# Gate scores taken from the output product, in an attention and expert kernel on one Trainium2 core

## What is computed

```python
x = x + xattn(layernorm(x), ctx, w_q, w_k, w_v, w_o, b_o)     # 16 heads of 64
y = layernorm(x)                                              # 64*128 tokens of 256
raw = softmax(y @ gate)                                       # 8 experts
g = the two largest of raw, divided by their sum
x = x + sum over those two experts e of g[e] * (relu(y @ W1[e] + b1[e]) @ W2[e] + b2[e])
```

## Time and profile before

| | |
|---|---|
| median of three runs | 1673.28 us (1673.21 to 1675.51) |
| profiled execution | 1680.6 us, span 1678.8 us, mean granted clock 0.995 |
| PE busy | 1638.5 us (98%) |
| DVE, ACT, POOL busy | 1249.7, 1219.1, 801.8 us (74%, 73%, 48%) |
| DMA | mean 85 GB/s |

### The profile page before, as it was taken

One profiled execution on the slowest core, in us unless ns is written; L12 is line 12 of the kernel. 1 busy time (PEld: TensorE's weight loads), 2 busy tenths in 40 slices (PEclk: granted clock), 3 DMA queues, 4 the chain that ended last, 5 costly groups with the idle time before them and its releaser, 6 DMA issues.

```text
span 1678.8 us, 45315 instructions
## 1 busy us (share of the span) xinstructions
PE 1638.5 (98%) x13932; PEld 1547.4 (92%) x13933; DVE 1249.7 (74%) x3302; ACT 1219.1 (73%) x3547; POOL 801.8 (48%) x888
## 2 busy tenths in 40 slices
PE   6999999999999999999999999999899999999997
PEld 6899999999999999999999999998899999999997
DVE  6777777777777777777777777776778777777775
ACT  6777777777777777777777777777666677777774
POOL 3334444444444444444444444444436555555555
PEclk9999999999999999999999999999999999999999
DMA  7121111122111111221111112211489655555554
GB/s 237 47 64 63 57 57 57 57 79 76 65 63 57 57 57 57 87 72 62 63 57 57 57 57 88 72 63 48 133 270 278 131 84 86 89 86 88 84 87 60
DMA packets 105755, 142.96 MB, mean 85 GB/s; under 512 B 12464, under 2 KB 88368, under 8 KB 105584
## 3 DMA queue, kind: packets, MB, share of 16 engines
q1 hardware_dynamic: 60672, 86.91, 15.8%
q0 software_dynamic: 26816, 37.32, 12.4%
q10 hardware_dynamic: 18224, 18.19, 3.9%
HBM read 75.00 MB, written 67.38 MB: 85 GB/s over the span
## 4 chain that ended last, share of the span: by engine, by line
issue 46%; POOL 20%; PE 12%; DVE 8%; DMA 6%; DVEq 3%; ACT 2%; POOLq 2%; ACTq 0%; SPq 0%
POOL lists L600 7%; PE bank_a L1284 6%; DMA out<-stage_room,number 5%; POOL prob L607 5%; DVE hid L1200 3%; POOL rstd L586 2%; DVE stage_room L1217 2%; POOL stage_room L633 2%; POOL stage_room L629 2%; PE bank_s L1284 2%; PE bank_t L1291 1%; PE bank_v L1317 1%; POOL out L669 1%; DVEq L1212 1%; POOLq L663 1%
## 5 line engine op out<-in xcount | busy, mean ns | idle before, releaser
L607 POOL TENSOR_TENSOR prob<-prob,inv 128x512 f32<-128x512 f32 x256 | 268.9, 1051 | 630.8 <-DVE inv L896 617.4
L713 ACT ACTIVATE prob<-bank_s,low 128x128 f32<-128x128 f32 x1024 | 363.1, 367 | 170.6 <-DVE low L891 129.0
L891 DVE TENSOR_REDUCE low<-bank_s 128x4 f32<-128x512 f32 x256 | 176.5, 690 | 253.3 <-PE bank_s L1284 253.1
L669 POOL DMA_INDIRECT out<-stage_room,number x142 | 232.0, 1634 | 53.5 <-issue 52.6
L713 ACT ACTIVATION_READ_ACCUMULATOR prob<-bank_s,low 128x1 f32 x1024 | 208.4, 204 | 0.0
L1291 PE MATMUL bank_t<-ident,prob 128*128 128x128 f32 x1024 | 164.5, 283 | 12.1 <-POOL prob L607 11.0
L919 DVE TENSOR_TENSOR kt_l<-bank_a,kt_h 64x512 fp32r<-64x512 f32 x256 | 173.2, 677 | 1.7
L822 ACT ACTIVATE hidt_h<-hid 128x512 fp32r<-128x512 f32 x142 | 89.8, 632 | 109.8 <-DVE hid L1200 105.2
L1284 PE MATMUL bank_s<-kt_l,qt_h 128*128 128x256 f32 x512 | 166.2, 325 | 0.0
L751 ACT ACTIVATE ot_h<-bank_v 128x512 fp32r<-128x512 f32 x128 | 76.5, 598 | 114.6 <-PE bank_v L1317 112.7
L706 ACT ACTIVATE probt<-bank_t 128x512 f32<-128x512 f32 x256 | 152.9, 597 | 8.3 <-PE bank_t L1291 7.0
(11 more groups left out here) (210 smaller groups left out, 5313.3 us busy)
## 6 DMA issues: line engine op xcount, KB each, us to landing
stage_room<-lists ACTq DMA_DIRECT2D x67, 265.0 KB
halves<-stage_room SPq DMA_DIRECT2D x32, 512.0 KB, 3.7
homes<-halves SPq DMA_DIRECT2D x8, 2048.0 KB, 10.1
xin<-in_x SPq DMA_DIRECT2D x32, 256.0 KB
stage_room<-in_x SPq DMA_DIRECT2D x32, 256.0 KB, 3.1
stage_room<-in_w SPq DMA_DIRECT2D x32, 256.0 KB, 3.8
out<-stage_room SPq DMA_DIRECT2D x32, 256.0 KB, 2.2
cin<-in_ctx SPq DMA_DIRECT2D x32, 128.0 KB
```

Of the source, the lines that this page charges most:

```text
L607: pool.tensor_tensor(prob[:, n % 4, :, :], prob[:, n % 4, :, :], wide(inv[:, n % 4, :], P), ALU.mult).then_inc(s_norm.sem, 1)
L669: pool.indirect_dma_start(out, bass.IndirectOffsetOnAxis(ap=number[:, u, b:b + 1], axis=0), ysum[:, u, b, :], None, compute_op=ALU.add).th ...
L713: e = act.activation(prob[:, n % 4, h, :], bank_s[n % 2][:, h * P:(h + 1) * P], ACT.Exp, bias=low[:, n % 4, h:h + 1], scale=-1.0, accum_ou ...
L891: dve.tensor_reduce(low[:, n % 4, :], bank_s[n % 2][:, :].rearrange("p (h k) -> p h k", h=4), AX.X, ALU.min).then_inc(s_low.sem, 1)
```

## The change

The gate scores of a pair are linear in the sums, up to the two numbers of the layer norm. The gate is first centred (`gate_c`, its column mean subtracted), so that the mean of a row drops out, and the scores become rstd times (x1 · gate_c). x1 is the output product plus the tokens plus the bias, so the kernel computes w_o · gate_c once (`wo_gate`, made in pass 0 in the place of `o1`, from a transposed w_o that a new 1 MB DMA brings) and hangs it to w_o as eight more columns: `o0` and `o1` have 264 moving columns for 256. The part of the tokens comes from eight small float32r products in the new `f0`, at the end of slot 7: stationary the 128x128 parts of `xt`, moving 16 columns of the gate's high and low parts. DVE rescales it (`x_gate`), POOL adds the bias's part.

```diff
 A_SLOTS:
-        [("q10", CUR), ("k10", CUR), ("l0", EARLIER)],
+        [("q10", CUR), ("k10", CUR)],
         [("o0", PREV)],
         [("k11", CUR), ("q11", CUR)],
-        [("f0", EARLIER), ("o1", PREV)],
-        [("v10", CUR), ("v11", CUR), ("t0", NEXT), ("t1", NEXT)],
+        [("o1", FROM0), ("t0", NEXT)],
+        [("v10", CUR), ("v11", CUR)],
...
-        [("y0", PREV), ("y1", PREV), ("k01", NEXT), ("v01", NEXT)],
+        [("k01", NEXT), ("v01", NEXT), ("f0", BOTH)],
 product, o:
+                    elif kind == "o" and isinstance(it, int) and it == 0:
+                        pe.wait_ge(wo_t_in, 16)
+                        for i in range(CHUNKS):
+                            for c in range(DC):
+                                last = pe.matmul(dst[:, i * E:(i + 1) * E], wo_t[:, c, i * P:(i + 1) * P], gate_c[:, c, :],
                                                 start=c == 0, stop=c == DC - 1, skip_group_check=True)
-                            last = three(dst[:, 0:D], [ot[s][:, k, c, :] for s in range(2)],
+                            last = three(dst[:, 0:WIDE], [ot[s][:, k, c, :] for s in range(2)],
 product, f0 (before the old four products of places):
+                        if has(it, NEXT):
+                            for b in range(2):
+                                part = dst[:, (4 + 2 * b) * E:(6 + 2 * b) * E]
+                                for c in range(DC):
+                                    for s in (1, 0):
+                                        last = pe.matmul(part, xt[s][:, c, b * P:(b + 1) * P],
                                                         gate_hl[:, c, :, :].rearrange("p s e -> p (s e)"),
...
+                        if has(it, PREV):
+                            last = places(it, dst)
 POOL:
-                        if n == 2 and has(it, EARLIER):
-                            ids(it)
+                        if n == 5 and has(it, PREV):
+                            ids(it)
-                        if n in (4, 5) and has(it, EARLIER):
-                            send(it, n - 4)
+                        if n in (1, 2) and has(it - 1, PREV):
+                            send(it - 1, n - 1)
 ACT:
-                        if n == 2 and has(it, EARLIER):
-                            numerators(it)
+                        if n == 6 and has(it, PREV):
+                            numerators(it, x1[:, :, D:])
                         if n == 4 and has(it, NEXT):
+                            wait(act, a_full, it, "v11")
 DVE:
-                            normalise(it, 1, x1, [xn2[:, b, :] for b in range(2)])
+                            rows_of(it)
+                        if n == 7 and has(it, PREV):
+                            gate_top(it)
+                            gate_weights(it)
+                def rows_of(it):
+                    gate_from(it)
+                    dve.wait_ge(sent, (it - 1) * 64 + 16)
+                    normalise(it, 1, x1, [rows[:, b, 0:D] for b in range(2)])
 SP:
                 def load_home(e):
+                    load_half(e, 0)
+                    sp.wait_ge(home_in[e], 16)
+                    load_half(e, 1)
```

More of the change, by code:

```diff
@@ L32 @@
 BIG = float(1 << 17)
-EARLIER, PREV, CUR, NEXT = "earlier", "prev", "cur", "next"
+PREV, CUR, NEXT = "prev", "cur", "next"
+BOTH, FROM0 = "both", "from0"
 class Signal:
@@ L69, in wait, with program @@
         engine.wait_ge(signal.sem, value - back)
-def program(nc, x, ctx, w_q, w_k, w_v, w_o, b_o, gate, w12, b1, b2, out):
+def program(nc, x, ctx, w_q, w_k, w_v, w_o, w_ot, b_o, b_oc, gate, w12, b1, b2, out):
     tokens, D = x.shape
@@ L1035, in body @@
                                 low_out(it, LAST[n][0])
-                            if name == "f0" and has(it, EARLIER):
-                                slots_of(it)
+                            if name == "f0" and has(made_in, PREV):
+                                slots_of(made_in)
                         if n == 4 and has(it, NEXT):
@@ L1240, in _ @@
                 relu(0, 0, 0)
-                normalise(PAIRS, 1, x1, [xn2[:, b, :] for b in range(2)])
+                rows_of(PAIRS)
                 relu(0, 0, 1)
@@ L1324, in product @@
                     kind, k = name[0], int(name[-1])
-                    wait(pe, a_done, it, name, A_BANKS if not isinstance(it, int) or it < PAIRS or name in ("o0", "o1")
-                         else 2 if kind in "lf" and it == PAIRS else 1)
+                    wait(pe, a_done, it, name, A_BANKS - 1 if isinstance(it, int) and it == PAIRS and kind == "f" else A_BANKS)
                     if kind == "t":
                         wait(pe, ln1_step, it, "ln1")
-                        for c in range(DC):
-                            last = pe.transpose(dst[:, c * P:(c + 1) * P], xn[:, k, c * P:(c + 1) * P], ident[:, :])
+                        for b in range(2):
+                            for c in range(DC):
+                                last = pe.transpose(dst[:, (2 * c + b) * P:(2 * c + b + 1) * P],
+                                                    xn[:, b, c * P:(c + 1) * P], ident[:, :])
                     elif kind == "q":
@@ L1333, in product @@
                         if k == 0:
-                            wait(pe, a_done, it if g == 0 else it - 1, "t1" if g == 0 else "q00")
+                            wait(pe, a_done, it if g == 0 else it - 1, "t0" if g == 0 else "q00")
                         for j in range(2):
@@ new lines, in product, with places @@
+                    last.then_inc(a_full.sem, 1)
+                def places(it, dst):
+                    wait(pe, route_step, it, "g_mask")
+                    pe.matmul(dst[:, 0:2 * E], upper[:, :], g_mask[:, :, :].rearrange("p b e -> p (b e)"),
+                              start=True, stop=False, skip_group_check=True)
+                    pe.matmul(dst[:, E:2 * E], all_ones[:, :], g_mask[:, 0, :], start=False, stop=True,
+                              skip_group_check=True)
+                    for b in range(2):
+                        last = pe.matmul(dst[:, 2 * E:3 * E], all_ones[:, :], g_mask[:, b, :], start=b == 0,
+                                         stop=b == 1, skip_group_check=True)
+                    return last
@@ L1407, in body, with gate_means, bias_scores @@
                                     pe.wait_ge(w_lo, V_READY)
-                                product(it, name)
+                                if name != "f0":
+                                    product(it, name)
+                                if isinstance(it, int) and it == -1 and name == "t0":
+                                    bias_scores()
                         if n in VALUES and has(it, VALUES[n][1]):
                             values(it, VALUES[n][0], n)
+                        if n == 7 and has(it, BOTH):
+                            product(it, "f0")
+                def gate_means():
+                    pe.wait_ge(gate_in, 32)
+                    pe.wait_ge(gate_made, 1)
+                    for c in range(DC):
+                        last = pe.matmul(bank_v[:, 0:E], prob[:, 0, 0, :], gate_sb[:, c, :], start=c == 0, stop=c == DC - 1,
+                                         skip_group_check=True)
+                    last.then_inc(gate_mean, 1)
+                def bias_scores():
+                    pe.wait_ge(gate_made, 2)
+                    for c in range(DC):
+                        last = pe.matmul(bank_v[:, E:2 * E], bo_col[:, c:c + 1].to_broadcast([P, P]), gate_c[:, c, :],
+                                         start=c == 0, stop=c == DC - 1, skip_group_check=True)
+                    last.then_inc(gate_mean, 1)
+                gate_means()
                 pe.wait_ge(made, 20)
@@ L1422, in turn_x @@
                         if j == 0:
-                            wait(pe, a_done, PAIRS - 1, "v10")
+                            wait(pe, a_done, PAIRS - 1, "v11")
                         elif j <= 2 * STEPS:
```

315 lines of the change are left out of this document (168 added, 147 removed).

## The result

On the chip of the first measurement the changed kernel took 1679.11 us (median of 8, 1676.24 to 1681.85) against 1673.87 of the kernel before: ratio 1.0031, 95% interval 1.0019 to 1.0044. (1673.87 is the median of the seven fast runs of eight; the eighth took 5535 us.) I had forecast 1657.5 and a range up to 1674; both are missed, and the sign too. The profiled executions hardly differ: 1680.0 us after (span 1678.3), 1680.6 before. On a second chip, with both kernels unedited, the kernel before took 1682.4 and the changed one 1680.2, ratio 0.9986 (0.9975 to 0.9997). So the first finding is that the kernel before has two speeds, by chip, and the changed kernel took nearly the same time on the two chips where it ran.

A forecast was written before the change was run, and what follows sets the result against it. PE was taken to bound the kernel. 29 looped passes at -0.65 us gave -18.9, once +3.1, together -15.8: profiled 1680.6 to 1664.8, median 1673.28 to 1657.5; range 1652 to 1674.

The forecast's parts named there:

- l0, f0, y: Work removed from PE's looped pass: l0 (slot 0) 0.84 us, f0 (slot 3) 0.18, y's transposes 0.44; together 1.46.
- Token products: Eight new small products at slot 7's end add 0.88 us a pass, 0.105 to 0.11 each; ends 0.2 and 1.6.
- the third: Rival: token products take up to 0.20 us each, not 0.11; +22 us, time 1680; chance 0.10.
- the fourth rival: Token products' loads are hidden, 0.03 us each; 20 us more gained, time 1637; chance 0.03.
- Columns: Eight more columns in 48 products add 3.7 ns a product, 0.18 us a looped pass.
- Wait in slot 5: PE's wait for t1's low part at q00's first product goes: 0.18 us a looped pass gained.
- Delay in slot 6: PE's wait before slot 6's transposes, behind DVE's late minimum, goes by parting indirect DMAs from load_x: 0.25 us a pass.
- Covers: Slack in the slots hides the work moved on DVE, ACT and POOL and DVE's new wait: all costed at nothing.
- Rivals: Five, among them: slot 6 delay stays, 1664.8 (chance 0.26); it moves to slot 4, 1673.5 (0.13); rows late, 1686 (0.06).
- Once: Costs and gains outside the looped passes (first passes, pass 31, tiles): +3.1 us together, of which pass 0 +4.1.

The follow-up runs named there:

- the trace of chip 8: Follow-up run of the kernel before, unedited, on a chip without the delay in slot 6: median 1670.83 us, profiled 1670.3.
- f0_behind_scores: Changed kernel with the twelve token and place products moved behind slot 0's scores of the next pass: 1661.73 us, ratio 0.9928 to the kernel before.
- qlo_over_branch: Changed kernel with token and place products at the next pass's head, plus POOL's subtraction q_lo moved from slot 7 into slot 0: 1664.59 us, ratio 0.9896.
- f0_over_branch: Changed kernel with the twelve token and place products moved from slot 7's end to the next pass's head: 1666.35 us, ratio 0.9961 to the kernel before.

## Why the prediction was wrong, step by step

The comparison is made with the trace of chip 8, as the first measurement was, by its time, on a chip of that speed. From that trace to the changed kernel's the span goes from 1668.5 to 1678.3 us, +9.8; the first measurement's medians and ratio give +5.2. The difference lies in the two executions: the one traced on chip 8 is 3.5 us below the median of the first measurement, the changed kernel's 0.9 above its own.

- **l0, f0, y.** Right: slot 0 fell by 0.85 (0.84 forecast), slots 3 and 4 add up to the forecast within 0.1 us, and slot 7 lasts 4.68 us in f0_behind_scores, where neither y nor f0 is left in it, 0.45 under the 5.13 of before (y: 0.44 forecast).
- **Token products.** Right as a price on PE (0.11 apart, 0.81 from the first start to the eighth; the third and the fourth rival are out), wrong as a price of the pass: at the end of slot 7 the mask was later than they.
- **Columns.** Mis-sized: slot 1, with 24 of the 48 products, grew by 0.02 us, so they cost 0.04 a pass and not 0.18.
- **Wait in slot 5.** Right: slot 5 fell by 0.18.
- **Delay in slot 6.** The step that failed first. It is gone from the trace as forecast (3.75 us), and its cause, the indirect DMAs beside the loads, was right as far as it was tested: moving them alone did the same on chip 3. But on the chip of the measurement, which by its time is one without the delay, there was nothing to remove: 7.3 us of the forecast's 15.8. The sentence that carried a profile's 7.3 us excess over the median into the forecast as a constant held the clue and used it wrongly: the excess was the delay.
- **Covers.** The step that failed worst. "DVE gets the search for the two best in slot 7" was costed at nothing, though PE's places wait for it and POOL is busy beside it: 0.20 us a pass (shown by qlo_over_branch). And what ends the loop's body was not asked at all: the branch, 0.44 us a pass (shown by f0_over_branch). Together they are 28 x 0.64 = 17.9 us, more than the whole forecast gain.
- **Rivals.** None of the five was the case. The third, slower and 1680, comes within 1 us of the measured 1679.1, but that is luck: its token products at 0.17 us or more were 0.11.
- **Once.** Forecast +3.1; in these two traces +7.8. First scores and pass 0 give +7.9 for the forecast +5.0; pass 1 +0.8 for +0.6; pass 30 -0.2; pass 31 and the way to the first tile's second layer +1.7 for -0.3 (-1.3 in slots 0 to 6, +3.0 from slot 7 on); the tiles behind it -2.4 for -2.2. The 32 records take 3.49 us (3.4 forecast).

The two large misses among these, in pass 0 and from slot 7 of pass 31, are TensorE's clock for the most part. The kernel before lasts 33.73 us in pass 0 where the clock stays at its upper level, 35.15 with one short stretch at the lower and 36.27 with two; the changed kernel 40.09 and 39.93 with two, and 38.51 with one (f0_behind_scores). Like against like that is +3.4 to +3.8 for the +4.1 that I had forecast. The mean granted clock of the stretch is 1.00 in the trace of chip 8 and 0.91 in the changed kernel's:

```profile
26.00:62.00 36.00, 30.83 (x257) 28.17 (x256) 24.80 (x50) 29.30 (x99) 11.68 (x12) 1.00 0.26 79
```

```profile
26.00:62.00 36.00, 31.67 (x240) 29.71 (x240) 21.97 (x46) 24.56 (x83) 7.56 (x10) 0.91 0.34 105
```

Most of these falls come right behind a wait of some 2 us for POOL's probabilities. The kernel before has such a wait near 30 us in all its four traces, and the clock fell behind it in two of them; so it differs by the execution, too. From slot 7 of pass 31 to the first tile's second layer it is the same: the kernel before takes 24.7 to 24.9 us in three traces with 6.8 us at the lower level and 27.8 in the fourth with 13.7; the changed kernel takes 27.7 with 13.7 (o0's 24 products alone 4.50 us), and f0_behind_scores, with no wait for the mask, 27.5 with 13.6. That the wait for the mask lengthened this way is therefore not shown.

Sum over passes 2 to 29 on a chip without the delay: forecast -0.65 a pass; without the slot 6 term -0.40; columns -0.14; branch +0.44, mask +0.20: +0.10. Measured are 37.03 - 36.96 = +0.07 by the means and 37.01 - 36.91 = +0.10 by the medians. PE in pass 0 of the changed kernel, the new records and the wait for POOL:

```profile
37.93 3.64 PE L1439 MATMUL bank_a<-gate_c,wo_t 128*128 128x8 f32 x32
...
48.93 0.66 PE L1364 MATMUL bank_t<-ident,prob 128*128 128x128 f32 x4 [2.25 <-POOL prob L638]
```

The account closes for the loop. For what happens once it closes in pass 0, within 0.7 us, when executions with the same clock are compared. How much of the unprofiled +5.2 us is the clock isn't shown stretch by stretch; the mean granted clock was 0.989 to 0.993 in the changed kernel's eight runs and 0.993 to 0.996 in the nine of the kernel before on chip 8. Why the changed kernel has more of the lower level stays open.

## What to carry to other kernels

Ask what instruction stands last in a loop's body on the engine that bounds it: here a branch was free behind a long queue of records and cost 0.44 us behind short products that had waited for a semaphore. Before small VectorE operations are put on a path that TensorE waits for, look at what POOL runs in that slot. And where a profile and the runs beside it differ by more than their scatter, explain the difference before taking a part of the profile for a gain.

## What was not expected of the hardware

- PE's loop branch, bare, costs 0.44 us a pass: a distance of 0.56 us in place of 0.12. The Trainium skill (Advanced Engine Details and Errata, Control Flow Timing) has a compare-and-branch at some 108 ns; the loss in these traces is four times that, and no run here shows what the rest consists of.
- A VectorE operation of 0.17 us on 16 elements took up to 0.92 us beside a POOL operation of 1.26 us, and 0.17 again when that was moved. One on 8 elements with a single tile as input was held as well.
- The same program, 1671 us on one chip and 1682 on another, with equal granted clocks (0.995 and 0.994): VectorE, idle, starts on the scores 0.32 us after the last of them has started or 1.01, in the slot behind the one where four loads and the indirect DMAs are issued.
- Half of a group of small products left out, 0.4 us of PE a pass: in one place no gain, in the other 0.03 us. What they cost depended on what else was late.
